# A four-layer graph kernel: count windows from chunk 404 on made of packs of 8 or 9 chunks with slots of their own

## The reference, cut to what matters

```python
x = LN(x + segment_sum(w[e] * x[src[e]], dst) @ W0.T)                     # layer 0
# layer 1: two graph convolutions, 256 -> 128 -> 64, with batch norm
h = x @ W1;  x1 = relu(BN(segment_sum(norm[e] * h[src[e]], dst) + b1))
h = x1 @ W2; x2 = relu(BN(segment_sum(norm[e] * h[src[e]], dst) + b2))
x = LN(x + relu(concat(x, x1, x2) @ Wfc + bfc))
x = LN(x + mlp((1 + eps) * x + segment_sum(w[e] * x[src[e]], dst)))       # layer 2
x = LN(x + relu(LN(segment_sum(norm[e] * h[src[e]], dst) + b)))           # layer 3
```

## Time and profile before

| | us |
|---|---|
| median of 3 runs | 3434.1 (3432.6 to 3437.4) |
| the profiled execution, its own time | 3437.4 |
| its span | 3436.1 |
| PE / DVE / ACT / POOL busy | 2833.6 / 2051.0 / 1009.4 / 2503.3 |
| mean DMA rate | 190 GB/s |

### The profile page before, as it was taken

The page is one execution under the profiler, slowest core; times in us unless marked ns, Lnnn a source line. Parts: engine busy times, 40 slices in busy tenths (PEclk is TensorE's granted clock), DMA queues, the critical chain, the costliest instruction groups (busy, mean ns, idle before and its releaser), DMA issues. The chain is left out here.

```text
span 3436.1 us, 59943 instructions
## 1 busy us (share of the span) xinstructions
PE 2833.6 (82%) x19203; PEld 2096.4 (61%) x19220; DVE 2051.0 (60%) x7385; ACT 1009.4 (29%) x2549; POOL 2503.3 (73%) x2237
## 2 busy tenths in 40 slices
PE   5989888888888869789968887678788875699995
PEld 4767666566777648444447774366676664466664
DVE  7899988887888638342253334433444564245557
ACT  4343444445666438100010003400111232001123
POOL 3888888887777666677747777777777774777773
PEclk9999999999999979899969996589999988799997
DMA  8777888888999889788847876755565554988884
GB/s 274 113 140 102 157 158 155 152 152 182 187 186 181 176 221 313 193 217 236 236 105 201 225 219 176 228 155 156 167 181 174 166 170 137 291 234 248 250 251 137
DMA packets 658433, 652.77 MB, mean 190 GB/s; under 512 B 87902, under 2 KB 606476, under 8 KB 656588
## 3 DMA queue, kind: packets, MB, share of 16 engines
q0 software_dynamic: 153600, 258.41, 37.7%
q1 hardware_dynamic: 430670, 331.83, 31.3%
q10 hardware_dynamic: 73854, 58.70, 5.4%
HBM read 434.19 MB, written 214.52 MB: 189 GB/s over the span
## 5 line engine op out<-in xcount | busy, mean ns | idle before, releaser
L1691 POOL DMA_INDIRECT A<-rows_buf,big x572 | 940.2, 1644 | 272.4 <-issue 155.3
L885 POOL DMA_INDIRECT rows_buf<-T,idx x888 | 851.7, 959 | 276.0 <-issue 273.9
L979 PE MATMUL PSA<-S,rows_buf 128*128 128x128 bf16 (+2 forms) x5904 | 585.8, 254 | 221.9 <-DMA rows_buf<-X,idx 103.8
L979 PEld LDWEIGHTS PSA<-S,rows_buf 128*128 128x128 bf16 (+2 forms) x5904 | 525.4, 143 | 303.8 <-DMA rows_buf<-X,idx 93.3
L1035 DVE TENSOR_TENSOR accT<-PSA,accT 128x256 f32 (+2 forms) x354 | 132.7, 375 | 837.8 <-PE PSA L979 830.8
L885 POOL DMA_INDIRECT rows_buf<-X,idx x528 | 508.9, 964 | 161.0 <-issue 157.6
L1381 PE MATMUL PSA<-XRS,rows_buf 128*128 128x256 f32 x1144 | 312.6, 397 | 3.9 <-DMA XRS<-in_xpad 3.9
L1547 DVE TENSOR_TENSOR accT<-PSA,accT 128x392 f32 (+5 forms) x366 | 239.2, 654 | 76.7 <-PE PSA L1478 41.4
L1393 ACT ACTIVATE rows_buf<-PSA 128x512 f32<-128x512 f32 x286 | 169.2, 594 | 225.9 <-PE PSA L1381 212.4
L1381 PEld LDWEIGHTS PSA<-XRS,rows_buf 128*128 128x128 f32 x1144 | 210.7, 197 | 30.4 <-issue 5.2
L796 ACT ACTIVATE accT<-accT,vec 128x500 f32<-128x500 f32 (+3 forms) x26 | 17.7, 693 | 668.4 <-DVE accT L794 668.3
(11 more groups left out here) (316 smaller groups left out, 5540.6 us busy)
## 6 DMA issues: line engine op xcount, KB each, us to landing
XRS<-Ad SPq DMA_DIRECT2D x400, 256.0 KB
Ad<-accT SPq DMA_DIRECT2D x224, 196.0 KB
XRS<-in_xpad SPq DMA_DIRECT2D x192, 128.0 KB, 4.1
Awd<-accT SPq DMA_DIRECT2D x48, 392.0 KB
A<-accT SPq DMA_DIRECT2D x9, 1600.0 KB
rows_buf<-T,idx POOLq DMA_INDIRECT x888
rows_buf<-A SPq DMA_DIRECT2D x24, 512.0 KB
accT<-A SPq DMA_DIRECT2D x24, 512.0 KB, 6.3
```

Source lines behind the costliest of these rows:

```text
L885: s_hg[slot(i)][j // 2].on(pool.indirect_dma_start(Gv(slot(i), j), None, table, bass.IndirectOffsetOnAxis(idx[:, c:c + 1], 0)), 16)
L979: last = pe.matmul(PS[bank_of(i)][0:F, W * h:W * h + W], Gv(slot(i), j)[:, o:o + F], hits[:, i % SRING, j, :], start=j + part == 0, stop=j ...
L1691: s_k[n].on(pool.indirect_dma_start(A, bass.IndirectOffsetOnAxis(tgt[:, c:c + 1], 0), G[:, i % RING, j, :], None, compute_op=ALU.add), 16)
```

## The change

From chunk 404 on (window 16) windows are no longer cut by how many targets they span. They are *packs*: 8 windows of 9 chunks with 14 slots each, then 8 windows of 8 chunks with 16 slots each (`PACKS`). Chunk number j of a pack has columns of its own in the window, from 14 j or 16 j on, and counts there from its own first target. No two chunks of a pack share a column.

So a unit's counts are copied into `Aw`, not added: DVE copies blocks 0 to 24, and ACT writes blocks 25 to 48 straight into `Aw`. `ABW`, the second add and the clearing of buffers fall away for packs. In layer 1 the columns of a pack no longer lie at one place, so `packed_quad` adds each chunk's 14 or 16 columns at the chunk's place, with a register loaded for each chunk (from `ubi`), four in a load.

There are now 16 windows and 16 packs, 32 in all, up to chunk 540: 8 quads in both passes of layer 1, and 60 gathered groups (135 to 194) in each. Layers 2 and 3 keep their windows.

```diff
-NWIN = 28
+NATURALS = 16
+PACKS = ((8, 9, 14), (8, 8, 16))
+NWIN = NATURALS + sum(m for m, _, _ in PACKS)
...
+    for m, k, _ in PACKS:
+        for _ in range(m):
+            b.append(b[-1] + k)
...
-    cost = lambda u: 1.15 + 0.67 * u.k if u.hot else 0.2 + 0.051 * u.n + u.k * (0.35 + 0.0128 * u.n)
+    cost = lambda u: 1.15 + 0.67 * u.k if u.hot else 1.35 if u.packed else 0.2 + 0.051 * u.n + u.k * (0.35 + 0.0128 * u.n)
...
+        def packed_quad(q):
+
+            if by_rows is None:
+                s_hdn.by(v, D0 + PQ * (q + 1))
+            else:
+                s_tp.by(v, T0 + q + 1)
+            bank = 2 + 2 * (q % pairs) if by_rows is None else 6
+            units = [(j, c) for j in range(per) for c in range(BND[per * q + j], BND[per * q + j + 1])]
+            for k, (j, c) in enumerate(units):
+                if k % LOADREGS == 0:
+                    lo = c - PACKED
+                    los = nc.values_load_multi_w_load_instructions(
+                        ubi[0:1, lo:min(lo + LOADREGS, BND[per * q + per] - PACKED)], engines=[ET.DVE], min_val=0, max_val=LAST,
+                        skip_runtime_bounds_check_because="held under LAST")[1]
+                slots = WIDTHS[per * q + j - NATURALS]
+                aw = acc(los[k % LOADREGS])[:, 0:slots]
+                at = 512 * bank + W * j + slots * (c - BND[per * q + j])
+                s_hacc.by(v)
+                s_hqa.by(v)
+                s_hqa.on(v.scalar_tensor_tensor(aw, PSA[0:F, at:at + slots], okf[0:F, 0:1], aw, ALU.mult, ALU.add))
...
+                if w >= NATURALS:
+                    s_ca.of(sp, ("unit", FINAL[w].at))
...
+            if u.packed:
+                sc.wait_ge(s_amw, NUW + u.half + 1)
+                if u.first:
+                    before = user_before(u.w)
+                    sc.wait_ge(s_aw[TURN[before] % 2], 16 * PARTS * (TURN[before] // 2 + 1))
+                got = PS[7][:, 0:(NT - FIRSTHALF) * u.n].rearrange("p (b s) -> p b s", s=u.n)
+                s_ca.mark(("unit", u.at), sc.activation(pack_slots(u)[:, FIRSTHALF:NT, :], got, ACT.Identity))
...
+            if u.packed:
+                v.wait_ge(s_ae, u.turns[0])
...
+                v.wait_ge(s_am, u.at + 1)
+                got = AB[:, 0:FIRSTHALF * u.n].rearrange("p (b s) -> p b s", s=u.n)
+                v.tensor_copy(pack_slots(u)[:, 0:FIRSTHALF, :], got).then_inc(s_ae, 1)
+                return
```

More of the change, by code:

```diff
@@ L53, in window_bounds @@
     b, last = [0], 0.0
-    for w in range(1, NWIN + 1):
+    for w in range(1, NATURALS + 1):
         c = E / 128 * math.sqrt((last + SPAN) / N)
@@ L81, in __init__ @@
         self.hot = w < HWIN
+        self.packed = w >= NATURALS
 def natural_units():
@@ L89, in natural_units @@
             us.append(Unit(c, k, next(w for w in range(NWIN) if c < BND[w + 1]), n))
+    for w in range(NATURALS, NWIN):
+        us += [Unit(c, 1, w, WIDTHS[w - NATURALS]) for c in range(BND[w], BND[w + 1])]
     for i, u in enumerate(us):
@@ L114 @@
 for i, u in enumerate(HALVED):
-    turns += [(u, 0)] + [(HALVED[i - 1], 1)] * (i > 0)
-turns.append((HALVED[-1], 1))
+    turns += [(u, 0)] + [(HALVED[i - 1], 1)] * (i > 0 and not HALVED[i - 1].packed)
 for u in UNITS:
@@ L126, in window_range, with sums_of @@
 def window_range(w):
-    at = N * (BND[w] * 128 / E) ** 2
-    return max(0, math.floor(at) - 125), min(LAST, math.ceil(at) + 125)
+    at, last = (N * (c * 128 / E) ** 2 for c in (BND[w], BND[w] if w < NATURALS else BND[w + 1] - 1))
+    return max(0, math.floor(at) - 125), min(LAST, math.ceil(last) + 125)
+def sums_of(q, per):
+    return sum(1 if w < NATURALS else BND[w + 1] - BND[w] for w in range(per * q))
 def unit_at(p):
@@ L179 @@
 DENSE0 = cleared_at(HWIN - 1, 3) + 1
-CLEARED = [w for w in ORDER if w >= HWIN and any(user_before(q) == w for q in range(NWIN))]
+CLEARED = [w for w in ORDER if w >= HWIN and any(user_before(q) == w for q in range(NATURALS))]
 FARBLOCK = window_range(HWIN)[0] // 128
@@ L495, in build @@
         least, most = window_range(w)
-        done = v.tensor_scalar(wb[:, lo:hi], cm[:, lo:lo + 1].broadcast_to([128, hi - lo]), float(least), float(most), ALU.max, ALU.min)
+        starts = cm[:, lo:lo + 1].broadcast_to([128, hi - lo]) if w < NATURALS else cm[:, lo:hi]
+        done = v.tensor_scalar(wb[:, lo:hi], starts, float(least), float(most), ALU.max, ALU.min)
     link(done)
     s_d.by(sc)
-    for w in range(NWIN):
-        first = sc.activation(bwi[0:1, w:w + 1], wb[0:1, BND[w]:BND[w] + 1], ACT.Identity)
-    s_q.on(first)
+    for w in range(NATURALS):
+        sc.activation(bwi[0:1, w:w + 1], wb[0:1, BND[w]:BND[w] + 1], ACT.Identity)
+    s_q.on(sc.activation(ubi[:, :], wb[0:1, PACKED:HOT], ACT.Identity))
     hot16 = cur16[:, 0:G0, :]
@@ L515, in scatter_rows @@
         link(v.tensor_scalar(spare[:, :, :], srcf[:, :, :], -1.0, pidx[:, 0:1], ALU.mult, ALU.add))
+    widths = [(lo, hi, n) for lo, hi, k, n in CLASSES]
+    widths += [(BND[w], BND[w + 1], WIDTHS[w - NATURALS]) for w in range(NATURALS, NWIN)]
     def unit_places_known():
@@ L526, in unit_places_known @@
             u += m
-        link(v.tensor_tensor(wb, wb, off, ALU.add))
+        link(v.tensor_tensor(wb[:, 0:PACKED], wb[:, 0:PACKED], off[:, 0:PACKED], ALU.add))
         s_rnd.on(v.tensor_tensor(wb, dstf[:, 0:HOT], wb, ALU.subtract))
@@ L1719, in additions @@
                 unit_out(u)
-                if u.halved and u.half:
+                if u.halved and u.half and not HALVED[u.half - 1].packed:
                     unit_out(HALVED[u.half - 1], 1)
-                if u is HALVED[-1]:
-                    unit_out(u, 1)
         equals(0)
```

40 lines of the change are left out of this document (27 added, 13 removed).

## The result

The changed kernel takes 3572.4 us (median of 4 runs, 3570.8 to 3576.6) against 3434.2 us: ratio 1.0394, 95% interval 1.0378 to 1.0411. It is slower by 138 us where the prediction said 95. 3572 is the upper end of its range, and above the 3500 to 3555 that it gave the forecast alone.

A forecast was written before the change was run, and what follows sets the result against it. SP's chain of single pieces was taken to bound layer 0 from 1051 us, POOL's gathers layer 1, with PE close. Layer 0 +52, first pass +31, second pass +12 make +95 on 3434.1: 3529 us, range 3466 to 3572.

The forecast's parts named there:

- Layer 0, +52: Layer 0 from about 911 us: SP's one-at-a-time pieces set the pace, 22.0 us a window, 354 us, ending at 1265.
- rival 2: Layer 0 costs little (20.0 us a window, +23), layer 1 adds at their low bound: 3475 us; chance 0.17.
- DVE's savings counted as nothing: Layer 0: 48 + 22 us of adds and clears removed on DVE count nothing, since SP doesn't wait for DVE.
- Rival 1: Faster: builder was the bound, DVE's 70 us count, windows in 16 us, 3364 us; chance 0.08 with weaker forms.
- First pass, +31: Layer 1, first pass: +5 with PE as bound, +13 for stalls at quads 4 to 6, +13 for quad 7 at the end.
- The adds' time at the end: End of each layer 1 pass: quad 7's 32 adds, 15 us, stand where all wait for them, +13.
- Base: Layer 1 passes without add costs: first +5, PE above POOL's 5.05 us a group; second -20, POOL staying the bound.
- Stalls: Layer 1: PE waits for DVE at packed quads 4, 5 and 6; +13 in the first pass, +20 in the second.
- Second pass, +12: Layer 1, second pass: POOL -20, PE ending some 20 us behind it, quad 7 in the tail +13; bounds 0 to +22.
- The sign that POOL would wait for PE in the first pass but not in the second: Layer 1, sign of being right: PE bounds the first pass, POOL stays the bound in the second.
- rival 3: The adds hide, SP doesn't: layer 1 gives +5 and -20, layer 0 +52, 3471 us; chance 0.06.
- rival 5: The clock: PE, in steps of 11 us, gets the lower clock more often, 10 to 30 us more, 3550 us; chance 0.15.

The follow-up runs named there:

- a_two: Changed kernel with two pieces of a window in flight instead of one: 3497.8 us, 1.0200 of the kernel before.
- a_28: Changed kernel with 12 packs instead of 16 (28 windows), pieces still one at a time: 3522.8 us, 1.0244 of the kernel before.
- b_two: Kernel before the change with two pieces of a window in flight: 3417.0 us, 0.9967 of before; run again 3416.8 us, 0.9951.
- a_one: Changed kernel, layer 1 adding each packed window once, 128 columns wide, instead of per chunk (sums not the reference's): 3481.9 us, 1.0140 of before.
- a_spread: Changed kernel with the adds of quads 4 to 6 spread over several groups, quad 7 in one piece: 3519.7 us, 1.0269 of before.

## Why the prediction was right in sign and short in size

**Layer 0, +52: right.** The bound was named rightly, SP's chain of pieces, and a_two and a_28 show it from two sides. Measured +61; the three other profiled executions with the same layer 0 gave 1445.3, 1445.5 and 1457.8, so +53 to +66. I took 22.0 us a window; 16 packs took (1273 - 913.7) / 16 = 22.5. A single piece hardly got faster with a DMA share of 0.79 in place of 0.87: 171.3 / 71 = 2.41 us of waiting, before 121.6 / 49 = 2.48. The Trainium skill ("DMA: Bandwidth & Descriptors", latency and other measured facts) says that a lighter load makes the fixed part of a transfer smaller; the trace is no more than compatible with it, by 0.07 us, and it isn't enough for the 20 us a window of rival 2.

**DVE's savings counted as nothing: right.** Rival 1 needed windows in 16 us. With the chain relieved a window takes 17.4, and even then the packed layer 0 isn't shorter than that of b_two: in a_two PE is busy 134.9 us of the stretch from 1051 to 1211, and DVE waits 80 us for PE at its copies (911 to 1200 us).

**First pass, +31, measured +46.** By a_one and the last rows of the passes it splits as follows. The adds' time at the end: 384.9 - 370.2 = 14.7 us from the last product to quad 7's last add, 2.0 in a_one: +12.7 for a forecast of +13. Base: +8.5 for +5. Stalls: the last product came 370.2 us into the pass, 345.7 in a_one, so +24.5 for +13: *this is the step that failed*. The waits themselves were 7.6, 5.7 and 2.2, in sum 15.4 us, close to the 3 x 4.5 that I took. What I left out is the time behind a wait. The clock was at half for 6.8 us each around the first two (from 1708.6 and from 1756.4 us). PE stood for part of that and worked through the last 4.2 and 5.4 us, at 1.06 instead of 0.59 us for two products. It was by then the bound and could win nothing back, and so lost about half of these 9.6 us, 4.8. Waits for pieces are 2 us more than in a_one. The last 2.6 us have nothing to do with the adds: at DVE's last add for a group ahead of the first packed quad, after was already at 233.0 us of the pass and a_one at 230.4, though their work up to there is the same. So the adds' stalls were 22 us for 13. The clock stood among the rivals for layer 0 alone. The Trainium skill ("TensorE: Matmul & The Clock Gate", on what is actually happening) says that the array falls back to half its clock when it has been idle; the trace agrees, it fell during the wait of 7.58 us. That the waits and the half clock belong together is shown: in the first pass both went with a_spread. How the 24.5 us divide is worked out from the trace, not tried.

**Second pass, +12, measured +36.** This lies outside its own bounds, 0 to +22. End: 17.3 us against 4.7 in a_one, +12.6 for +13. Stalls: last product at 351.7 us, 320.5 in a_one, +31.2 for +20; the waits were 10.4, 10.1 and 5.4 us where I had 9, 9 and 5. The clock was at half from 2114.8 and from 2162.6 us, 10.2 us each, and twice more around the third wait; PE worked through 16 us of it in all, and lost some 8. The step that failed in the first pass failed here too. Base: -7.9 for -20: *the other step that failed*. I had PE at 4.9 us a group, just under POOL's 5.05, and let POOL keep its gain. In a_one PE took 5.20. Of the difference 0.2 are its waits for pieces, which my sum had left out (10.5 us in 18 waits over the pass, 3.6 us before); 0.1 isn't accounted for. So it fell 13.6 us behind POOL even without the adds. A bound that by the sum is only 3% under another is not hidden by it. The sign that POOL would wait for PE in the first pass but not in the second came half: 40.7 us in the first, 15.0 in the second, 11.9 of it once near the end.

**Adds:** 0.24 us and 0.43 apart forecast, 0.233 and 0.43 measured; a quad 16.9 us for 17. By the Trainium skill's table ("VectorE: DVE Perf Modes", TRN2 errata) the estimate was 0.14 us; the measurement is 0.09 longer, and the rows decided rightly.

Against rival 1 stand a_28 and a_two, against rival 3 a_one. Of rival 5 the mechanism came true in layer 1, where it wasn't forecast, and only weakly in layer 0 (clock 0.94 in both stretches, 1.00 and 0.95 before). The sum missed by 43 us, and layer 0 and both passes missed to the same side; that 3572 still lies at the end of the range is owed to the width left for upper bounds and for a slow clock, not to the forecast's terms.

## What to carry to other kernels

When a change adds units to a queue that issues one transfer at a time, price it by the queue, even if every engine gets emptier; and before paying for fewer instructions elsewhere try a second transfer in flight, which took two semaphores here and returned 74 us. Many small adds in one piece can cost more than the waits that they cause: here TensorE was still at half clock when it went on after waits of 5.4 to 10.4 us, so spread them over the loop's turns and leave the shortest batch for the end. When two engines are within a few per cent of each other, count on no gain from relieving one of them until the other's small waits are in its sum.

## What was unexpected of the hardware

PE came out of five waits of 5.4 to 10.4 us for DVE at half its clock and worked on at it for 3 to 6 us, so that such a wait cost a seventh to a half more than its own length; after one of 2.2 us it did not. Four 196 KB pieces took 9 us one by one and 4 to 5 us with two in flight, where the DMA share had been 0.79 to 0.82 and rose to 0.91 to 0.96. And the same kernels ran 10 to 11% longer in two of five jobs, with an unchanged layer 0 and later layers slowed, which turned a comparison of 0.5% round: a verdict of that size on this kernel holds for the job in which it was taken.
